# First-pass values of a graph-attention kernel: DVE and ACT in turn on two tiles, POOL left out

## The chip, the cores and the metric

The kernel runs on one core of a Trainium2 chip. The metric is the device time of one execution in microseconds (us). The kernel before takes 3360.18 us, the median of three executions between 3354.19 and 3361.27 us.

The core's engines are TensorE (PE, with its weight loads shown as PEld), VectorE (DVE), ScalarE (ACT), GpSimd (POOL) and SyncE (SP, which only issues DMAs here). They run their own instruction streams and meet at semaphores.

## The reference

Four graph layers over 4096 nodes with 256 features. Layers 0 and 1 are graph attention with four heads of 64 columns; layer 2 is a wide attention with gates; layer 3 is attention with one score per node. Each layer's output is added to `x` and normalised.

```python
h = jnp.einsum('nf,hfd->hnd', x, W)
s_src = jnp.einsum('hnd,hd->hn', h, a1)
s_dst = jnp.einsum('hnd,hd->hn', h, a2)
e = jax.nn.leaky_relu(s_src[:, :, None] + s_dst[:, None, :], 0.01)
e = jnp.where(adj[None, :, :] == 0, -jnp.inf, e)
alpha = jax.nn.softmax(e, axis=-1)
out = jnp.einsum('hij,hjd->hid', alpha, h)
```

A leaky relu of a sum has two exponentials, one for each sign. So the kernel computes the softmax numerator as two masked sums over `j`, one with `exp(s_dst)` where the sum of scores is above zero, one with `exp(slope * s_dst)` where it is not. What is multiplied by the masks, `h` times one of the two exponentials, is called "values" in the kernel. Layer 3 has a single exponential and so one kind of values.

## The kernel before

Nodes are laid out as 128 partitions by T = 32 tiles. Layers 0, 1 and 3 run attention in four passes of 64 columns (`p`), each over eight groups of 512 target nodes (`g`), each in eight units (`k`). Layer 2 (`dense2`) has its own code, which the change does not touch.

**The values.** PE multiplies fp8 masks of zeros and ones by bf16 values. To keep fp32 accuracy each value is split into three bf16 parts. `value_parts` (line 462) makes them for `n` tiles of one kind: copy the exponential beside the products (line 467), multiply `h` by it into `big` (468), cast `big` to the first part (472), subtract it from `big` into `rest` (475), cast `rest` to the second part (478), subtract that into the third part (481). Each step waits for the one before. A chunk is CHUNK = 8 tiles; a kind has FIRST_CHUNKS = 4 chunks. A chunk is 128 x 520 elements.

**Who makes them.** The values of pass 0 cannot be made before the scores and exponentials of the layer exist, so they stand between the dense product and the attention. In layers 0 and 1, DVE makes all four chunks of kind 1 (line 1438) and the last chunk of kind 0 (`rest_of_first_values`, line 1318), with the temporary `vtmp_dve`; POOL makes the other three chunks of kind 0 (`first_values`, line 535, in `vtmp_pool`). In layer 3 DVE makes three chunks and POOL one. `POOL_CHUNKS` holds the split. The values of passes 1 to 3 are made by POOL in the slack of the pass before (line 595, half-size pieces, 128 x 260).

**What starts the attention.** PE waits for DVE's chunks (`s_vfirst`, line 992) and POOL's (`s_vals`, lines 981 and 999), and then for the masks of unit 0 (`s_sides`, line 958). The masks: ACT makes `above` for a unit with four relus (line 760), two units ahead, after copying the pass's scores into `kpass` (line 745); DVE takes the unit's adjacency bits (`edge`, line 1503), ANDs them with `above` (`pos`, 1509) and XORs (`neg`, 1512). In layer 3 there is no `above`; line 1500 makes the whole mask. DVE evacuates the banks of the group before at line 1454; in layer 0's first pass PE waits for that at the first group too, because a single half of the banks is used there and the packing of the adjacency matrix shares the pass. That packing takes six groups: SP loads 1 MB halves of a row block (line 350), DVE converts them (1212), PE packs (945), DVE stores (1218). SP's next load waits for the conversion of the half in the same buffer.

POOL also turns sums into quotients (lines 553 and 568 to 576), after it has made the group's values for the next pass. DVE's evacuation waits for the quotient of a group earlier (line 1451). Before each attention POOL runs one `PARTITION_ALL_REDUCE` (line 533).

The order on every engine is that of the program; there is no planner.

Of the kernel before, what the change touches and what calls it, by code (L numbers as in the profile page):

```python
# [6 lines left out]
ALU = mybir.AluOpType  # L7
# [10 lines left out]
P = 128  # L18
# [5 lines left out]
H = 4  # L24
D = F // H
# [15 lines left out]
POOL_CHUNKS = {0: 3, 1: 3, 3: 1}  # L41
# [17 lines left out]
def values_before(l):  # L59

    return sum(POOL_CHUNKS[m] + (H - 1) * NG for m in TURN if m < l)


def first_values_until(l):

    return sum(FIRST_CHUNKS - POOL_CHUNKS[m] for m in TURN if m <= l)

# [54 lines left out]
def gnn_kernel(nc, A, out, last_layer=3):  # L122

    with ExitStack() as ctx:
# [155 lines left out]
        s_vfirst = sem("dve_values_made")  # L280
        s_vals = sem("values_made")
# [202 lines left out]


        @block.gpsimd
        def _(pool):
# [47 lines left out]
            def first_values(l):  # L535
                if l < 3:
                    pool.wait_ge(s_exps, l + 1)
                else:
                    pool.wait_ge(s_emul, 1)
                with pool.Fori(0, POOL_CHUNKS[l]) as c:  # L540
                    chain.enter(c, VALUE_LINKS)
                    value_parts(pool, chain, vtmp_pool, 0, c * CHUNK, CHUNK, 0, 0).then_inc(s_vals, 1)
                chain.leave(POOL_CHUNKS[l])

# [35 lines left out]
            def attention(l):  # L580
                kinds = 2 if l < 3 else 1
                per_group = VALUE_LINKS * kinds + (3 if l < 3 else 2)
                for p in range(H if l < 3 else H - 1):

                    links = per_group - (0 if p < H - 1 else VALUE_LINKS * kinds)
                    if p < H - 1:

                        pool.wait_ge(s_unit, p * UNITS + (CREDIT + TURN[l] * H * UNITS))
                    with pool.Fori(0, NG // 2) as gg:
                        for par in range(2):  # L590
                            g = gg * 2 + par
                            chain.enter(g, links)
                            if p < H - 1:
                                for kind in range(kinds):
                                    made = value_parts(pool, chain, vtmp_pool, kind, g * GT, GT, p + 1, 1 - p % 2)
                                made.then_inc(s_vals, 1)
                            quotient(l, p, g, par)
                    chain.leave(NG)
# [77 lines left out]
            for l in range(last_layer + 1):  # L676
# [7 lines left out]
                if l != 2:  # L684
                    first_values(l)
                    attention(l)
# [7 lines left out]
        def _(act):  # L694
# [29 lines left out]
            def stats(l):  # L724
# [12 lines left out]
                else:  # L737
                    act.activation(emul[:, 0, 0, :], emul[:, 0, 0, :], ACT.Exp).then_inc(s_exps, 1)

# [147 lines left out]
            for l in range(last_layer + 1):  # L887
# [17 lines left out]
                stats(l)  # L905
                if l < 2:
                    attention(l)
# [8 lines left out]
        def _(pe):  # L916
# [62 lines left out]
            def one_pass(l, slot, p):  # L979

                pe.wait_ge(s_vals, p * NG + (values_before(l) + POOL_CHUNKS[l]))
# [8 lines left out]
            def attention(l):  # L990
# [8 lines left out]
                pe.wait_ge(s_vals, POOL_CHUNKS[0])  # L999
# [181 lines left out]
        def _(dve):  # L1181
# [136 lines left out]
            def rest_of_first_values(l):  # L1318

                with dve.Fori(POOL_CHUNKS[l], FIRST_CHUNKS) as c:  # L1320
                    chain.enter(c - POOL_CHUNKS[l], VALUE_LINKS)
                    value_parts(dve, chain, vtmp_dve, 0, c * CHUNK, CHUNK, 0, 0).then_inc(s_vfirst, 1)
                chain.leave(FIRST_CHUNKS - POOL_CHUNKS[l])
# [75 lines left out]
            def stats(l):  # L1399
# [9 lines left out]
                if l == 3:  # L1409
# [12 lines left out]
                    rest_of_first_values(l)  # L1422
# [15 lines left out]
                with dve.Fori(0, FIRST_CHUNKS) as c:  # L1438
                    chain.enter(c, VALUE_LINKS + 1)
                    value_parts(dve, chain, vtmp_dve, 1, c * CHUNK, CHUNK, 0, 0).then_inc(s_dve, 1)  # L1440
                    dve.wait_ge(s_dve, chain.next())
                chain.leave(FIRST_CHUNKS)
                rest_of_first_values(l)
# [308 lines left out]
```

## Time and profile before

| | us |
|---|---|
| median of three executions | 3360.18 |
| lowest, highest | 3354.19, 3361.27 |
| the profiled execution | 3357.18 |
| its span in the trace | 3355.4 |
| its mean granted TensorE clock | 0.961 |

| engine | busy us | share of the span | instructions |
|---|---|---|---|
| PE | 3011.8 | 90% | 26664 |
| PEld | 2751.1 | 82% | 26664 |
| DVE | 2278.4 | 68% | 4091 |
| ACT | 1914.1 | 57% | 3380 |
| POOL | 1226.3 | 37% | 1640 |

Of the chain of work that ended last, PE has 73% of the span, DVE 15%, issue 5%, DMA 3% and POOL 2%.

In the rows below, "busy" is the time in which an engine worked on an instruction, and the number in brackets is the idle time of the engine just before the instruction, with what ended it. "issue" is idle time in which the engine waited for nothing that the profile shows. Names left and right of "<-" are the tiles written and read; `rings` holds DVE's temporary and the masks, `values` holds the bf16 parts. [...] Times are microseconds from the span's start. The stretches of rows 1 are the first values of layers 0, 1 and 3, from DVE's first copy to its first mask.

### The profile page before, as it was taken

Reading aid. Unit: us, or ns where it says so; the run is one execution under the profiler, and the core shown is the slowest. Engines: PE = TensorE matmul, PEld = TensorE weight load, DVE = VectorE, ACT = ScalarE, POOL = GpSimd, SP = SyncE. Lnnn points to the kernel's source line nnn. Section 1 sums busy time; section 2 is a strip of 40 time slices with the busy share of each in tenths; the row PEclk is TensorE's granted clock in tenths of the full one; section 3 lists DMA queues with packets and bytes.
Section 4 is the critical chain, followed back from the end, with each engine's and each line's share of the span. In section 5 each row is a group of like instructions: output and inputs, shape, how many; then the busy total and the mean of one; then the engine's idle time right before and its main releaser. Section 6 shows DMA issues by size and latency. Waiting matters only on the chain.

```text
span 3355.4 us, 74122 instructions
## 1 busy us (share of the span) xinstructions
PE 3011.8 (90%) x26664; PEld 2751.1 (82%) x26664; DVE 2278.4 (68%) x4091; ACT 1914.1 (57%) x3380; POOL 1226.3 (37%) x1640
## 2 busy tenths in 40 slices
PE   6588899999955999999997999999999998569997
PEld 5587899999945999999995787887887886359997
DVE  4888788887777888888776555655655554454447
ACT  4455798889845898898884454444454443320000
POOL 2433456551214555545212013223223232324443
PEclk9799999999987999999998999999999998789999
DMA  7465000000100000000010000000000000000001
GB/s 258 177 243 205 10 13 11 12 13 13 61 0 11 13 13 11 12 13 10 12 40 7 9 2 4 4 1 4 4 1 4 1 1 2 0 1 0 0 0 50
DMA packets 42286, 104.58 MB, mean 31 GB/s; under 512 B 9904, under 2 KB 23472, under 8 KB 33968
## 3 DMA queue, kind: packets, MB, share of 16 engines
q1 hardware_dynamic: 42160, 102.92, 9.1%
q8 instruction: 77, 1.26, 0.2%
q14 instruction: 49, 0.40, 0.0%
HBM read 98.51 MB, written 4.39 MB: 31 GB/s over the span
## 4 chain that ended last, share of the span: by engine, by line
PE 73%; DVE 15%; issue 5%; DMA 3%; POOL 2%; ACT 1%; DVEq 1%; SPq 0%; POOLq 0%; ACTq 0%
PE bank L970 16%; PE bank L967 16%; PE bank L1014 14%; PE bank L1052 11%; PE bank L973 10%; DVE sums L1454 4%; DVE rings L1509 3%; PE bank L931 2%; DMA arena<-in_adj_dram 2%; DVE rings L1512 2%; PE bank L1041 2%; PE bank L1028 1%; PE bank L945 1%; DVE rings L1503 1%; DVE arena L1212 1%
## 5 line engine op out<-in xcount | busy, mean ns | idle before, releaser
L967 PE MATMUL bank<-values,rings 128*128 128x195 bf16 x8192 | 1418.4, 247 | 138.0 <-DVE rings L1512 79.0
L760 ACT ACTIVATE above<-srow,kpass 128x512 fp8e4<-128x512 f32 x2048 | 1292.9, 709 | 294.3 <-DVE rings L1512 278.6
L970 PE MATMUL bank<-values,rings 128*128 128x195 bf16 x8192 | 1418.6, 249 | 0.0
L967 PEld LDWEIGHTS bank<-values,rings 128*128 128x128 fp8e4 x8192 | 809.2, 99 | 157.2 <-issue 155.8
L970 PEld LDWEIGHTS bank<-values,rings 128*128 128x128 fp8e4 x8192 | 787.1, 96 | 1.1
L1509 DVE TENSOR_TENSOR rings<-rings,above 128x512 uint32<-128x512 uint32 x512 | 385.1, 752 | 237.2 <-PE bank L970 190.5
L778 ACT ACTIVATE values<-srow,cmul 128x512 f32<-128x512 f32 x256 | 205.9, 814 | 433.3 <-PE bank L1052 432.3
L1052 PE MATMUL bank<-hv,values 128*128 128x257 f32 x1792 | 423.8, 382 | 9.5 <-DVE values L1388 9.5
L1512 DVE TENSOR_TENSOR rings<-rings 128x512 uint32<-128x512 uint32 x512 | 408.6, 798 | 17.5
L1052 PEld LDWEIGHTS bank<-hv,values 128*128 128x128 f32 x1792 | 336.9, 191 | 80.5 <-issue 25.5
L973 PE MATMUL bank<-values,rings 128*128 128x195 bf16 x4096 | 349.3, 248 | 23.0 <-DVE rings L1500 23.0
L973 PEld LDWEIGHTS bank<-values,rings 128*128 128x128 fp8e4 x4096 | 348.6, 98 | 23.9 <-issue 23.4
L553 POOL TENSOR_TENSOR quot<-sums,cmul 128x260 f32<-128x260 f32 x64 | 43.8, 684 | 762.0 <-DVE sums L1454 762.0
L1503 DVE TENSOR_SCALAR rings<-packed 128x512 uint32 (+1 forms) x512 | 309.9, 605 | 0.7 <-DVE values L481 0.6
L1500 DVE TENSOR_SCALAR rings<-packed 128x512 uint32 (+1 forms) x256 | 113.3, 443 | 179.7 <-PE bank L973 177.8
L1388 DVE SCALAR_TENSOR_TENSOR values<-values,cmul,rings 128x512 f32<-128x512 f32 x256 | 193.1, 761 | 47.4 <-ACT values L778 46.4
L619 POOL TENSOR_SCALAR zrow<-zrow 128x1 f32<-128x1 f32 x96 | 39.1, 407 | 465.4 <-DVE zrow L1575 465.4
L1454 DVE TENSOR_REDUCE sums<-bank 128x130 f32<-128x390 f32 (+1 forms) x396 | 168.0, 486 | 15.8 <-PE bank L970 14.0
L1014 PE MATMUL bank<-arena,above 128*128 128x256 f32 (+1 forms) x512 | 176.0, 492 | 2.3 <-ACT above L842 2.3
L931 PE MATMUL bank<-weights,values 128*128 128x264 f32 (+1 forms) x512 | 141.8, 437 | 26.3 <-ACT values L699 25.9
L931 PEld LDWEIGHTS bank<-weights,values 128*128 128x128 f32 x512 | 108.8, 218 | 53.7 <-ACT values L699 33.7
L1014 PEld LDWEIGHTS bank<-arena,above 128*128 128x128 f32 x512 | 98.0, 192 | 60.0 <-issue 49.2
(177 smaller groups left out, 3505.4 us busy)
## 6 DMA issues: line engine op xcount, KB each, us to landing
arena<-in_adj_dram SPq DMA_DIRECT2D x64, 1024.0 KB, 5.7
srow<-src_dram SPq DMA_DIRECT2D x72, 256.0 KB, 3.2
x<-in_x_dram SPq DMA_DIRECT2D x1, 4096.0 KB, 14.3
out_dram<-x SPq DMA_DIRECT2D x8, 512.0 KB, 2.9
arena<-in_L_gnn_fe_w_dram SPq DMA_DIRECT2D x2, 512.0 KB, 10.0
arena<-in_L_gnn_W_hz_dram SPq DMA_DIRECT2D x1, 1024.0 KB, 10.4
arena<-in_L_gnn_g_w_dram SPq DMA_DIRECT2D x1, 1024.0 KB, 11.6
weights<-in_L_gnn_W_dram SPq DMA_DIRECT2D x3, 256.0 KB, 3.3
```

The lines of the kernel that those rows point to most:

```text
L760: last = act.activation(above[:, k % 2, q, :], srow[:, par, :], ACT.Relu, scale=BIG, bias=kpass[:, slot, q * BITS + k:q * BITS + k + 1], s ...
L778: act.activation(w2[:, m % DEPTH, :], srow[:, g % 2, :], ACT.Relu, scale=b_col[:, jt:jt + 1], bias=c_neg[:, jt:jt + 1]).then_inc(E.relu, 1)
L931: last = pe.matmul(bank[2 + i][:, 0:width], xT[:, i, k, :], weights[:, k, 0:width], start=(k == 0), stop=(k == 1))
L967: pe.matmul(acc[:, 0:KW], pos[:, k % 2, q, :].bitcast(FP8)[:, rows], v[:, 0:KW], start=first, stop=final, skip_group_check=True)
L970: last = pe.matmul(acc[:, KW:2 * KW], neg[:, k % 2, q, :].bitcast(FP8)[:, rows], v[:, KW:2 * KW], start=False, stop=final, skip_group_chec ...
L973: last = pe.matmul(acc[:, 0:KW], edge[:, k % 2, q, :].bitcast(FP8)[:, rows], v[:, 0:KW], start=first, stop=final)
L1014: last = pe.matmul(dst, lhsT[k], rhs[k], start=(k == 0), stop=(k == len(lhsT) - 1))
L1052: last = pe.matmul(bank[it][:, 0:VW], w2[:, m % DEPTH, it * P:(it + 1) * P], hv[:, q * BITS + k, :], start=(k == 0 and q == 0), stop=False)
L1454: last = dve.tensor_reduce(sums[:, slot, it, 0:kinds, :], parts, AX.X, ALU.add)
L1503: dve.tensor_scalar(edge[:, r], words, shift[0], ONE, shift[1], ALU.bitwise_and)\
L1509: dve.tensor_tensor(pos[:, r], edge[:, r], above[:, r].bitcast(U32), ALU.bitwise_and)\
L1512: dve.tensor_tensor(neg[:, r], edge[:, r], pos[:, r], ALU.bitwise_xor).then_inc(s_sides, 1)
```

## The change

The first pass's values are made without POOL. `first_values` on DVE goes through the chunks in pairs, the even one in `vtmp_dve` and the odd one in `vtmp_pool`, eight chunks (both kinds) in layers 0 and 1 and four in layer 3. DVE copies the exponential, multiplies, and later makes the two subtractions. ACT makes the two casts of each chunk in `first_casts`, between `stats` and `attention` in its program. Three new semaphores carry the turn: `s_vbig` (multiplied), `s_vcast` (cast), `s_vrest` (rest made). The loops over the chunks are written out in Python, so their instructions stand in line instead of in a hardware loop. POOL waits in `attention` for `s_vfirst`, since DVE now uses its temporary. PE waits for `s_vfirst` alone.

```diff
--- before.py
+++ after.py
@@ -38,7 +38,6 @@
 EPS = 1e-5
 CHUNK = 8
 FIRST_CHUNKS = T // CHUNK
-POOL_CHUNKS = {0: 3, 1: 3, 3: 1}
 UNITS = NG * BITS
 PACKED_FIRST = QUADS
 PACKING = (T - PACKED_FIRST) // GT
@@ -58,12 +57,17 @@
 
 def values_before(l):
 
-    return sum(POOL_CHUNKS[m] + (H - 1) * NG for m in TURN if m < l)
+    return sum((H - 1) * NG for m in TURN if m < l)
+
+
+def first_chunks(l):
+
+    return FIRST_CHUNKS * (2 if l < 3 else 1)
 
 
 def first_values_until(l):
 
-    return sum(FIRST_CHUNKS - POOL_CHUNKS[m] for m in TURN if m <= l)
+    return sum(first_chunks(m) for m in TURN if m <= l)
 
 
 
@@ -278,6 +282,7 @@
         s_exps = sem("exps_made")
         s_emul = sem("layer3_weights_made")
         s_vfirst = sem("dve_values_made")
+        s_vbig, s_vcast, s_vrest = sem("values_multiplied"), sem("values_cast"), sem("values_rest")
         s_vals = sem("values_made")
         s_srow = [sem("srow_loaded0"), sem("srow_loaded1")]
         s_above = sem("above_made")
@@ -482,6 +487,14 @@
 
         VALUE_LINKS = 4
 
+        def chunk_of(c):
+
+            return (vtmp_dve, vtmp_pool)[c % 2], c // FIRST_CHUNKS, c % FIRST_CHUNKS * CHUNK
+
+        def first_part(kind, j0, i):
+
+            return values[:, 0, j0:j0 + CHUNK, kind * KW + i * C:kind * KW + (i + 1) * C]
+
 
         @block.gpsimd
         def _(pool):
@@ -531,16 +544,6 @@
                 n = H if l < 2 else 1
                 pool.wait_ge(s_pmax, l + 1)
                 pool.partition_all_reduce(smax[:, 1, 0:n], smax[:, 0, 0:n], P, RMAX).then_inc(s_max, 1)
-
-            def first_values(l):
-                if l < 3:
-                    pool.wait_ge(s_exps, l + 1)
-                else:
-                    pool.wait_ge(s_emul, 1)
-                with pool.Fori(0, POOL_CHUNKS[l]) as c:
-                    chain.enter(c, VALUE_LINKS)
-                    value_parts(pool, chain, vtmp_pool, 0, c * CHUNK, CHUNK, 0, 0).then_inc(s_vals, 1)
-                chain.leave(POOL_CHUNKS[l])
 
             def quotient(l, p, g, par):
 
@@ -580,6 +583,7 @@
             def attention(l):
                 kinds = 2 if l < 3 else 1
                 per_group = VALUE_LINKS * kinds + (3 if l < 3 else 2)
+                pool.wait_ge(s_vfirst, first_values_until(l))
                 for p in range(H if l < 3 else H - 1):
 
                     links = per_group - (0 if p < H - 1 else VALUE_LINKS * kinds)
@@ -682,7 +686,6 @@
                     stage_x()
                 global_max(l)
                 if l != 2:
-                    first_values(l)
                     attention(l)
             if last_layer == 2:
                 dense2()
@@ -736,6 +739,19 @@
                     act.activation(c, c, ACT.Exp).then_inc(s_exps, 1)
                 else:
                     act.activation(emul[:, 0, 0, :], emul[:, 0, 0, :], ACT.Exp).then_inc(s_exps, 1)
+
+            def first_casts(l):
+
+                before = first_values_until(l) - first_chunks(l)
+                for pair in range(0, first_chunks(l), 2):
+                    for c in (pair, pair + 1):
+                        vtmp, kind, j0 = chunk_of(c)
+                        act.wait_ge(s_vbig, before + c + 1)
+                        act.activation(first_part(kind, j0, 0), vtmp[:, 0], ACT.Copy).then_inc(s_vcast, 1)
+                    for c in (pair, pair + 1):
+                        vtmp, kind, j0 = chunk_of(c)
+                        act.wait_ge(s_vrest, before + c + 1)
+                        act.activation(first_part(kind, j0, 1), vtmp[:, 1], ACT.Copy).then_inc(s_vcast, 1)
 
             def attention(l):
 
@@ -903,6 +919,8 @@
                     with act.Fori(0, QUADS) as q:
                         dense(l, q)
                 stats(l)
+                if l != 2:
+                    first_casts(l)
                 if l < 2:
                     attention(l)
             if last_layer == 2:
@@ -978,7 +996,7 @@
 
             def one_pass(l, slot, p):
 
-                pe.wait_ge(s_vals, p * NG + (values_before(l) + POOL_CHUNKS[l]))
+                pe.wait_ge(s_vals, p * NG + values_before(l))
                 pe.nop(nofuse=True)
                 with pe.Fori(0, NG // 2) as gg:
                     for par in range(2):
@@ -996,7 +1014,6 @@
                             one_pass(l, slot, pp * 2 + slot)
                     return
 
-                pe.wait_ge(s_vals, POOL_CHUNKS[0])
                 for begin, end in ((0, PACKING), (PACKING, NG)):
                     with pe.Fori(begin, end) as g:
 
@@ -1315,12 +1332,28 @@
                 dve.tensor_reduce(scores[:, H, ds(q * QT, QT)], low, AX.X, ALU.add).then_inc(s_dve, 1)
                 dve.wait_ge(s_dve, chain.next())
 
-            def rest_of_first_values(l):
-
-                with dve.Fori(POOL_CHUNKS[l], FIRST_CHUNKS) as c:
-                    chain.enter(c - POOL_CHUNKS[l], VALUE_LINKS)
-                    value_parts(dve, chain, vtmp_dve, 0, c * CHUNK, CHUNK, 0, 0).then_inc(s_vfirst, 1)
-                chain.leave(FIRST_CHUNKS - POOL_CHUNKS[l])
+            def first_values(l):
+
+                before = first_values_until(l) - first_chunks(l)
+                for pair in range(0, first_chunks(l), 2):
+                    both = (pair, pair + 1)
+                    for c in both:
+                        vtmp, kind, j0 = chunk_of(c)
+                        big = vtmp[:, 0]
+                        e = emul[:, kind, 0:1, j0:j0 + CHUNK].rearrange("p a n -> p n a")
+                        dve.tensor_copy(big[:, :, D:C], e)
+                        dve.tensor_tensor(big[:, :, 0:D], h[:, j0:j0 + CHUNK, 0:D], e.to_broadcast([P, CHUNK, D]),
+                                          ALU.mult).then_inc(s_vbig, 1)
+                    for c in both:
+                        vtmp, kind, j0 = chunk_of(c)
+                        dve.wait_ge(s_vcast, 2 * (before + c - c % 2) + c % 2 + 1)
+                        dve.tensor_tensor(vtmp[:, 1], vtmp[:, 0], first_part(kind, j0, 0), ALU.subtract)\
+                            .then_inc(s_vrest, 1)
+                    for c in both:
+                        vtmp, kind, j0 = chunk_of(c)
+                        dve.wait_ge(s_vcast, 2 * (before + c - c % 2) + c % 2 + 3)
+                        dve.tensor_tensor(first_part(kind, j0, 2), vtmp[:, 1], first_part(kind, j0, 1), ALU.subtract)\
+                            .then_inc(s_vfirst, 1)
 
                 dve.wait_ge(s_vfirst, first_values_until(l))
 
@@ -1419,7 +1452,7 @@
                     dve.tensor_copy(emul[:, 0, 0, :], emul[:, 0, 1, :]).then_inc(s_emul, 1)
                     chain.settle()
                     dve.wait_ge(s_emul, 1)
-                    rest_of_first_values(l)
+                    first_values(l)
                     return
 
                 z, az, m = (zrow[:, i] for i in range(3))
@@ -1435,12 +1468,7 @@
                 chain.settle()
 
                 dve.wait_ge(s_exps, l + 1)
-                with dve.Fori(0, FIRST_CHUNKS) as c:
-                    chain.enter(c, VALUE_LINKS + 1)
-                    value_parts(dve, chain, vtmp_dve, 1, c * CHUNK, CHUNK, 0, 0).then_inc(s_dve, 1)
-                    dve.wait_ge(s_dve, chain.next())
-                chain.leave(FIRST_CHUNKS)
-                rest_of_first_values(l)
+                first_values(l)
 
             def evacuate(l, half, slot, count):
```

## Rows read from the trace of the kernel before

**Rows 1.** By stretch: length, busy PE, PEld, DVE, ACT, POOL; clock, DMA share, GB/s.
```profile
84.35:110.55 26.20, 0.00 (x0) 0.00 (x0) 20.69 (x30) 5.01 (x8) 13.44 (x15) 0.50 0.24 92
1022.23:1048.64 26.41, 0.00 (x0) 0.00 (x0) 21.19 (x30) 5.01 (x8) 15.78 (x17) 0.50 0.07 20
2974.46:2988.65 14.19, 0.00 (x0) 0.00 (x0) 11.52 (x19) 0.00 (x0) 6.60 (x8) 0.50 0.00 0
```

**Rows 2.** Timeline (start, duration, engine, line, operation), layer 0, DVE's first chunk.
```profile
84.35 0.17 DVE L467 COPY rings<-emul 128x8 f32 x1 [1.09 <-ACT cmul L736]
...
84.50 0.69 DVE L468 TENSOR_TENSOR rings<-hv,emul 128x512 f32 x1
85.41 0.43 DVE L472 CAST values<-rings 128x520 f32 x1 [0.22 <-DVE rings L468]
...
85.95 0.70 DVE L475 TENSOR_TENSOR rings<-rings,values 128x520 f32<-128x520 f32 x1
```

**Rows 3.** Timeline, layer 1, DVE and POOL both making values.
```profile
1040.16 1.14 POOL L475 TENSOR_TENSOR vtmp_pool<-vtmp_pool,values 128x520 f32<-128x520 f32 x1
1040.50 1.36 DVE L481 TENSOR_TENSOR values<-rings,values 128x520 f32 x1 [0.20 <-DVE values L478]
```

**Rows 4.** Instructions of ACT by line and shape (busy us, mean ns): nearest to a cast.
```profile
L760 ACT ACTIVATE above<-srow,kpass 128x512 fp8e4<-128x512 f32 x2048 | 1292.9, 709 | 294.3 <-DVE rings L1512 278.6 <-DMA srow<-src_dram 4.3 <-ACT kpass L745 3.4
...
L868 ACT ACTIVATE values<-values 128x512 f32<-128x512 f32 x16 | 9.9, 618 | 15.4 <-DVE values L1688 15.4
...
L704 ACT ACTIVATE x<-values 128x1024 f32<-128x1024 f32 x2 | 2.1, 1048 | 0.0
```

**Rows 5.** Timeline, layer 3: DVE to ACT and back.
```profile
2973.06 0.19 DVE L1408 TENSOR_TENSOR emul<-scores,smax 128x32 f32<-128x32 f32 x1 [0.55 <-POOL smax L533]
...
2973.29 0.23 ACT L738 ACTIVATE emul<-emul 128x32 f32<-128x32 f32 x1 [3.51 <-DVE emul L1408]
2973.62 0.40 DVE L1416 TENSOR_TENSOR emul<-emul,zrow 128x32 f32<-128x32 f32 x3 [0.28 <-ACT emul L738]
```

**Rows 6.** Waits of ACT (total us, times, longest), relus after the kpass copy.
```profile
ACT above L760 <- ACT kpass L745: 3.4, 6, 0.6
```

**Rows 7.** Timeline of ACT, layer 0: four relus of one unit.
```profile
113.75 2.56 ACT L760 ACTIVATE above<-srow,kpass 128x512 fp8e4<-128x512 f32 x4 [22.89 <-DVE rings L1512]
```

**Rows 8.** Timeline, layer 0, from the values to PE.
```profile
111.28 1.35 DVE L1509 TENSOR_TENSOR rings<-rings,above 128x512 uint32<-128x512 uint32 x1 [0.21 <-DVE rings L1503]
...
113.58 1.96 DVE L1454 TENSOR_REDUCE sums<-bank 128x130 f32<-128x390 f32 x4
...
115.89 0.32 PE L967 MATMUL bank<-values,rings 128*128 128x195 bf16 x1 [35.56 <-DVE sums L1454]
```

**Rows 9.** Timeline, layer 1, from the values to PE.
```profile
1049.28 1.45 DVE L1509 TENSOR_TENSOR rings<-rings,above 128x512 uint32<-128x512 uint32 x1 [0.21 <-DVE rings L1503]
...
1052.04 0.32 PE L967 MATMUL bank<-values,rings 128*128 128x195 bf16 x1 [33.13 <-DVE rings L1512]
```

**Rows 10.** Timeline of DVE, layer 1, masks with POOL nearly quiet.
```profile
1057.00 0.69 DVE L1509 TENSOR_TENSOR rings<-rings,above 128x512 uint32<-128x512 uint32 x1 [0.45 <-ACT above L760]
1057.72 0.77 DVE L1512 TENSOR_TENSOR rings<-rings 128x512 uint32<-128x512 uint32 x1
```

**Rows 11.** Timeline, layer 3, from the values to PE.
```profile
2988.65 0.97 DVE L1500 TENSOR_SCALAR rings<-packed 128x512 uint32 x2 [0.60 <-DVE values L481]
...
2989.22 5.95 PE L973 MATMUL bank<-values,rings 128*128 128x195 bf16 x36 [23.03 <-DVE rings L1500]
```

**Rows 12.** Timeline of SP, layer 0, first loads after the values.
```profile
116.85 20.34 SPq L350 DMA_DIRECT2D arena<-in_adj_dram  x6
```

**Rows 13.** Waits of POOL (total us, times, longest).
```profile
POOL quot L568 <- DVE sums L1454: 165.3, 32, 12.7
...
POOL vtmp_pool L468 <- issue: 25.9, 5, 10.6
```

**Rows 14.** Waits of DVE on nothing that the profile shows.
```profile
DVE lnst L1250 <- issue: 3.8, 1, 3.8
```

## Prediction, made before the changed kernel was run

> **What bounds the kernel now.** I read the chain of work that ended last first: PE has 73% of the span and DVE only 15%, so making DVE cheaper is worth nothing inside a pass. Then the busy time by stretch. In three stretches PE has no matmul at all: 26.20 us in layer 0, 26.41 us in layer 1 and 14.19 us in layer 3 [rows 1]. These are the first pass's values, and nothing else is ready for PE. DVE is busy for 20.69, 21.19 and 11.52 us of them, so what ends them is DVE's own series of steps. Whatever is cut from DVE's series, up to PE's first matmul, is cut from the time, and the stretches occur once each. Last, the timeline shows what stands between DVE's last value and PE: PE begins at 115.89, 1052.04 and 2989.22 [rows 8, 9, 11], which is 31.54, 29.81 and 14.76 us after DVE's first copy (84.35, 1022.23 and 2974.46, the starts of the stretches in [rows 1]).
>
> **Prices of the steps.** On DVE a copy starts at 84.35 and its multiply at 84.50, ends at 85.19; a subtraction is 0.70 and a cast 0.43 [rows 2]. That is DVE without POOL. With POOL at work a subtraction took 1.36 beside POOL's 1.14 [rows 3]; this extra goes, since POOL makes nothing in the stretch. Instructions that don't depend on each other overlap a little: ACT's four relus of 0.709 need 2.56 instead of 2.84 [rows 4, 7], 0.09 less at each seam. I take 0.08 on DVE too and, at the far end, zero. ACT's cast isn't in the trace. 128 x 512 without a per-partition bias is 0.618 and 128 x 1024 is 1.048 [rows 4]; 520 elements come to 0.62 us. The bounds are 0.43 (DVE's own cast) and 0.71 (a relu with its bias [rows 4]). A hand-over: DVE ends at 2973.25, ACT starts at 2973.29; ACT ends at 2973.52, DVE starts at 2973.62 [rows 5]. So 0.04 and 0.10, and 0.57 (3.4 / 6 [rows 6]) as the far end. I take 0.04 to 0.06, as loops and their register work fall away.
>
> **A pair of chunks, step by step.** From its first copy at 0: multiplies end at 0.84 and 1.59. ACT casts 0.88 to 1.50 and 1.63 to 2.25. DVE subtracts 1.56 to 2.26 and 2.31 to 3.01. ACT casts the rests 2.30 to 2.92 and 3.05 to 3.67. DVE subtracts the third parts 2.98 to 3.68 and 3.73 to 4.43. The next pair starts at 4.35; I take 4.4 a pair. DVE has 3.9 us of work in it, so little is left to win; ACT has 2.5. Layers 0 and 1 have four pairs: DVE ends at 3 x 4.4 + 4.43 = 17.6, ACT's last cast at 3 x 4.4 + 3.67 = 16.9. Layer 3 has two: DVE ends at 8.8.
>
> **The wait that the change adds.** ACT's casts stand ahead of its relus. Before, ACT made eight relus for units 0 and 1 (5.01 us [rows 1]) while DVE made values; they cost nothing. Behind the last cast now stand the kpass copy and the relus of unit 0, and DVE's `pos` waits for them. 16.87, 0.2 for the copy, 0.57 to the first relu [rows 6], 2.56 for four [rows 7]: `pos` starts at 20.2 instead of 17.6 + 1.0. This costs 1.6 us in each of layers 0 and 1. The relus of unit 1 end at 22.8; `pos` of unit 1 wants them only after unit 0's matmuls are under way, so they stay hidden. Before, `pos` started at 111.28 - 84.35 = 26.93 and 1049.28 - 1022.23 = 27.05.
>
> **From the masks to PE.** `pos` and `neg` take 0.69 and 0.77 with POOL quiet, 1.49 from start to end [rows 10]; before, `pos` alone was 1.35 and 1.45 beside POOL [rows 8, 9]. Layer 1: 20.2 + 1.49 = 21.7 instead of 29.81, 8.1 us won. Layer 0: DVE also evacuates first; from that instruction's start (113.58) to PE is 2.31, so 21.6 + 2.3 = 23.9 instead of 31.54, 7.6 us won. Layer 3: no relus; 8.83 + 0.60 + 0.57 [rows 11] = 10.0 instead of 14.76, 4.8 us won.
>
> **Whether it is carried to the end.** After the values of layer 0 the adjacency loads set the pace, but SP's next load was issued at 116.85, after DVE's first conversion [rows 12], so the stream of loads starts earlier with DVE. After that every stage waits for the one before. I find no absolute time in the program.
>
> **What moves on POOL.** POOL now waits for `s_vfirst`, and behind that stand the values of pass 1 and the quotients. Its first multiply after the all-reduce waits for nothing visible, 10.6 us at the longest, 25.9 in all [rows 13]. Before, this ran beside DVE's values; now it starts after them. In layers 0 and 1 POOL is then at its pass-1 values at 17.6 + 10.6 = 28.2 or earlier, about when it got there before, when it had three chunks to make first. In layer 3 it is about 16, 6 us after PE's start. There POOL idles 165.3 / 32 = 5.2 us in each group before a quotient [rows 13], and that quotient is wanted a group later. So I cost it at nothing; if the cover were gone, it would be up to 3 us in layer 3. [...]
>
> **The sum.** 7.6 + 8.1 + 4.8 = 20.5 us. The profiled execution took 3357.18 (span 3355.4 and 1.8 around it), 3.0 under the median of the three. From the profiled execution it is 3336.7, from the median 3339.7. I say 3338.5, 0.65% less.
>
> **Own range of the forecast.** A pair could be 4.2 (casts at 0.43 leave DVE's own work and the hand-overs) or 5.2 (casts at 0.71 and 0.15 more in each of four hand-overs). Three pairs and a tail in two layers, two in the third: some ten pairs' worth, less for the smaller steps. That is 2 us more or 8 us less won: 3334.7 to 3344.7 from the profiled execution, up to 3347.7 from the median.
>
> **Rivals.** *Hand-overs as dear as the dearest.* Four hand-overs of 0.57 in a pair [rows 6] make it 6.4 us. Three pairs and three hand-overs more cost 7.5 us in each of layers 0 and 1, and 4 us in layer 3: 19 of the 20.5 are gone, 3355.7 to 3358. For it: it is a real row. Against it: that row has a loop's register work in it, and [rows 5] cross between the same two engines at 0.04 and 0.10. Chance 0.07.
> *Layer 0's share isn't carried.* If the load stream, not DVE, sets the end of the first pass, 7.6 us are lost: 3344 to 3347. For it: the loads set the pace there. Against it: their start follows DVE. Chance 0.10.
> *No overlap.* If the two chunks of a pair really run in series, a chunk is 0.84 + 2 x 0.62 + 2 x 0.70 + 4 x 0.05 = 3.7 us; eight are 29.6, and with the relus behind them PE starts 5.4 - 1.0 us later in two layers and 1.1 in layer 3: 10 us slower, 3367 to 3370. This is also where the change wouldn't do what it says. Against it: the program's order interleaves them. Chance 0.02.
> [...] Chance 0.05. [...]
>
> **How the numbers follow.** The forecast has 0.76, the rivals 0.07, 0.10, 0.02 and 0.05. A measurement of this kernel tells some 0.2% (6.7 us) from no change. Faster: 0.76 + 0.10 = 0.86. Same: 0.07. Slower: 0.07. The range is 3331 to 3349: the forecast's own range from both bases, 3 us wider below, and it holds the second rival.
>
> **What would show it.** In the timeline of the changed kernel: pairs of 4.4 us; ACT casts of 0.62; DVE subtractions of 0.70 all through; `pos` of unit 0 ending a wait for ACT's relu in layers 0 and 1; PE's first matmul 23.9, 21.7 and 10.0 us after DVE's first copy; POOL's stall of 7 to 11 us after that, without anybody behind it. The forecast is wrong if casts are over 0.8 us, if DVE stands between the steps for more than 0.3, or if PE waits for sums that wait for POOL.

## The result, and the profile after

The changed kernel takes 3335.36 us (median of four, 3329.51 to 3337.34) where the kernel before took 3358.14 us in the same session. The ratio is 0.993 with a 95% interval of 0.9912 to 0.9948: 22.8 us less. Run once more in another session it took 3334.19 against 3356.62, ratio 0.9938 (0.9924 to 0.9951). All times here and below are medians of the executions, without a single one of 5385.11 us of the run "POOL kept busy", in which the granted clock was 0.556.

The page's engines and its chain of work that ended last. POOL made 42 instructions fewer, ACT 40 more; DVE's count is the same but for two.

```profile
PE 3012.7 (90%) x26664; PEld 2751.2 (82%) x26664; DVE 2266.7 (68%) x4093; ACT 1939.8 (58%) x3420; POOL 1188.9 (36%) x1598
...
PE 73%; DVE 14%; issue 6%; DMA 3%; ACT 2%; POOL 2%; DVEq 1%; SPq 0%; POOLq 0%; ACTq 0%
```

The shares say little: they are those of before within a point or two. The change is in three short stretches, which answer to [rows 1] (columns as there).

```profile
84.87:101.88 17.01, 0.00 (x0) 0.00 (x0) 16.48 (x32) 10.67 (x18) 0.00 (x0) 0.50 0.40 145
1015.65:1032.81 17.16, 0.00 (x0) 0.00 (x0) 16.49 (x32) 10.83 (x18) 0.12 (x1) 0.50 0.11 31
2959.92:2968.97 9.05, 0.00 (x0) 0.00 (x0) 8.29 (x17) 5.15 (x8) 0.19 (x1) 0.50 0.00 0
```

They are 9.2, 9.2 and 5.1 us shorter, and DVE is busy for 16.48 of 17.01 us, where it was busy for 20.69 of 26.20. POOL has left them. One pair of chunks in the timeline of layer 1:

```profile
1015.65 0.18 DVE L1344 COPY rings<-emul 128x8 f32<-128x8 f32 x1 [0.88 <-ACT cmul L739]
1015.73 0.69 DVE L1345 TENSOR_TENSOR rings<-hv,emul 128x512 f32<-128x512 f32 x1
1016.33 0.17 DVE L1344 COPY vtmp_pool<-emul 128x8 f32<-128x8 f32 x1
1016.40 0.68 DVE L1345 TENSOR_TENSOR vtmp_pool<-hv,emul 128x512 f32<-128x512 f32 x1
1016.45 0.65 ACT L750 ACTIVATE values<-rings 128x520 bf16<-128x520 f32 x1 [0.83 <-DVE rings L1345]
1017.12 0.65 ACT L750 ACTIVATE values<-vtmp_pool 128x520 bf16<-128x520 f32 x1
1017.13 0.70 DVE L1350 TENSOR_TENSOR rings<-rings,values 128x520 f32<-128x520 f32 x1
1017.80 0.70 DVE L1350 TENSOR_TENSOR vtmp_pool<-vtmp_pool,values 128x520 f32<-128x520 f32 x1
1017.87 0.64 ACT L754 ACTIVATE values<-rings 128x520 bf16<-128x520 f32 x1
1018.54 0.64 ACT L754 ACTIVATE values<-vtmp_pool 128x520 bf16<-128x520 f32 x1
1018.54 0.70 DVE L1355 TENSOR_TENSOR values<-rings,values 128x520 bf16<-128x520 f32 x1
1019.21 0.70 DVE L1355 TENSOR_TENSOR values<-vtmp_pool,values 128x520 bf16<-128x520 f32 x1
1019.83 0.17 DVE L1344 COPY rings<-emul 128x8 f32<-128x8 f32 x1
```

DVE has next to no idle time between these rows, and the next pair starts after 4.18 us. ACT has a part in the pace: its casts of a pair start 0.67 us apart, and each of DVE's subtractions starts 0.03 us after the end of the cast that it needs (1017.10 and 1017.13, 1017.77 and 1017.80). So the two engines go in step, each with 0.64 to 0.70 us per instruction. The end of the same stretch, with the wait that the change adds:

```profile
1031.59 0.21 ACT L761 ACTIVATE kpass<-kscores 128x32 f32 x1
...
1032.38 9.91 ACT L776 ACTIVATE above<-srow,kpass 128x512 fp8e4<-128x512 f32 x16 [0.58 <-ACT kpass L761]
...
1032.81 0.43 DVE L1531 TENSOR_SCALAR rings<-packed 128x512 uint32 x1 [0.39 <-DVE values L1355]
1034.97 0.69 DVE L1537 TENSOR_TENSOR rings<-rings,above 128x512 uint32<-128x512 uint32 x1 [1.73 <-ACT above L776]
```

DVE has its bits at 1033.24 and waits 1.73 us for ACT's relus; before, the same instruction had its usual 0.21 [rows 9]. PE's first matmuls of layers 0, 1 and 3, each from the timeline of PE:

```profile
107.85 0.32 PE L985 MATMUL bank<-values,rings 128*128 128x195 bf16 x1 [26.79 <-DVE sums L1482]
```
```profile
1036.53 0.32 PE L985 MATMUL bank<-values,rings 128*128 128x195 bf16 x1 [24.01 <-DVE rings L1540]
```
```profile
2969.54 2.77 PE L991 MATMUL bank<-values,rings 128*128 128x195 bf16 x16 [17.69 <-DVE rings L1528]
```

From DVE's first copy that is 22.98, 20.88 and 9.62 us, where it was 31.54, 29.81 and 14.76 [rows 8, 9, 11]. This number, "PE's start", is what I compare from here on.

### The profile page after: what moved, and what is told of

The parts are those of the page before. It is cut to its first block, busy times and chain, and to the rows that moved or that the text cites. A ratio compares the mean times of both kernels' runs of the same rounds, so it can differ in the third digit from the quotient of the medians.

```text
span 3335.5 us, 73845 instructions
## 1 busy us (share of the span) xinstructions
PE 3012.7 (90%) x26664; PEld 2751.2 (82%) x26664; DVE 2266.7 (68%) x4093; ACT 1939.8 (58%) x3420; POOL 1188.9 (36%) x1598
## 4 chain that ended last, share of the span: by engine, by line
PE 73%; DVE 14%; issue 6%; DMA 3%; ACT 2%; POOL 2%; DVEq 1%; SPq 0%; POOLq 0%; ACTq 0%
PE bank L988 16%; PE bank L985 16%; PE bank L1031 14%; PE bank L1069 11%; PE bank L991 10%; DVE sums L1482 4%; DVE rings L1537 3%; DMA arena<-in_adj_dram 2%; DVE rings L1540 2%; PE bank L1058 2%; PE bank L949 1%; PE bank L1045 1%; DVE rings L1531 1%; DVE arena L1229 1%; PE bank L963 1%
```

## The experiments

The table has PE's start in microseconds in each kernel's trace, the sum over the three layers against before (76.1), and the time against the kernel before on the same chip.

| kernel | layer 0 | layer 1 | layer 3 | sum | sum against before | time against before |
|---|---|---|---|---|---|---|
| before, first and second trace | 31.54, 31.54 | 29.81, 29.79 | 14.76, 14.75 | 76.1 | | |
| changed, first and second trace | 22.98, 22.97 | 20.88, 20.87 | 9.62, 9.62 | 53.5 | -22.6 | -22.8, -22.4 |
| all on DVE, pairs | 25.21 | 23.28 | 11.93 | 60.4 | -15.7 | -16.7 |
| all on DVE, old loops | 36.51 | 34.78 | 15.84 | 87.1 | +11.0 | +10.6 |
| POOL keeps its chunks | 31.34 | 28.66 | 13.74 | 73.7 | -2.4 | -2.6 |
| one chunk at a time | 34.25 | 32.15 | 15.25 | 81.7 | +5.5 | +4.7 |
| POOL kept busy | 28.76 | 26.71 | 10.98 | 66.5 | -9.7 | -13.2 |
| POOL warmed up | 23.10 | 21.01 | 9.89 | 54.0 | -22.1 | -22.2 |
| relus in ACT's gaps | 21.30 | 19.36 | 9.62 | 50.3 | -25.8 | -26.5 |

**Casts on DVE too.** ACT's `first_casts` goes; DVE makes the casts in the same pairs.

```diff
+for c in both:
+    dve.wait_ge(s_vbig, before + c + 1)
+    dve.tensor_copy(first_part(kind, j0, 0), vtmp[:, 0]).then_inc(s_vcast, 1)
...
-    first_casts(l)
```

> POOL makes no first values, as in the changed kernel, but DVE makes the casts too and ACT none. Theory (the change is two gains that add: POOL out of the way, casts off DVE): a pair of chunks is 4.17 + 4 x 0.35 = 5.6 us; ACT's relus are hidden again. PE starts 24.9 us after DVE's first copy in layer 1, 27.0 in layer 0, 12.4 in layer 3, which is 10.8 us in all more than in the changed kernel and 11.8 less than in the kernel before. Rival 1 (the casts on ACT are the whole gain): the time of the kernel before, 22 us over the changed one. Rival 2 (POOL's quiet is the whole gain): within 3 us of the changed kernel.

Measured: 3339.74 against 3356.46, ratio 0.9947 (0.9931 to 0.9964). Both rivals fall, and the theory's split is wrong in size: 4 to 6 us over the changed kernel by the times and 6.9 by PE's starts, not 10.8. In its timeline (layer 0) DVE shows no idle time and casts follow each other after 0.34 us:

```profile
86.06 0.42 DVE L1348 CAST values<-rings 128x520 bf16<-128x520 f32 x1
86.40 0.42 DVE L1348 CAST values<-vtmp_pool 128x520 bf16<-128x520 f32 x1
...
86.74 0.69 DVE L1352 TENSOR_TENSOR rings<-rings,values 128x520 f32<-128x520 f32 x1
87.35 0.69 DVE L1352 TENSOR_TENSOR vtmp_pool<-vtmp_pool,values 128x520 f32<-128x520 f32 x1
```

Its subtractions start 0.61 apart, where in the changed kernel they follow ACT's casts and start 0.67 apart, so a pair takes 5.16 and not 5.6. The casts on ACT shorten the stretch by 4 us in each of layers 0 and 1, of which the relus behind them take back 1.7 and 1.5.

**The old loops on DVE, POOL out.** The kernel before, with `POOL_CHUNKS` at zero and POOL waiting for `s_vfirst`. DVE has the same work as in the run above, in hardware loops, one step behind the other.

```diff
-POOL_CHUNKS = {0: 3, 1: 3, 3: 1}
+POOL_CHUNKS = {0: 0, 1: 0, 3: 0}
...
+pool.wait_ge(s_vfirst, first_values_until(l))
```

> The kernel before with one edit: DVE makes all chunks (eight, four in layer 3) in its old hardware loops, one step waiting for the other, and POOL makes none and waits for the values, as in the changed kernel. With the run in which DVE did everything in pairs written out, this parts POOL's quiet from the order of the steps. In the trace of before, chunks of kind 1 without POOL took 4.5, 4.3, 4.25 and 4.2 us in the loop, those of layer 3 3.65. Theory A (the order of the steps and the missing loop are the larger part): the values take about 32 us in layers 0 and 1 and 14.6 in layer 3; PE starts about 36.8, 33.7 and 15.8 us after DVE's first copy, 10 us in all later than in the kernel before and 26 later than with the pairs written out on DVE alone. Rival B (POOL's quiet is what the gain came from): at least as fast as the kernel before, PE's starts within 2 us in all of 60.4, those of the pairs on DVE alone.

Measured: 3366.92 against 3356.37, ratio 1.0028 (1.0014 to 1.0042), and PE's starts within 1.1 us of theory A. Rival B falls. One chunk in layer 0:

```profile
84.60 0.43 DVE L472 CAST values<-rings 128x520 f32 x1 [0.22 <-DVE rings L468]
85.14 0.70 DVE L475 TENSOR_TENSOR rings<-rings,values 128x520 f32<-128x520 f32 x1
86.05 0.43 DVE L478 CAST values<-rings 128x520 f32 x1 [0.21 <-DVE rings L475]
86.74 0.70 DVE L481 TENSOR_TENSOR values<-rings,values 128x520 f32 x1 [0.26 <-DVE values L478]
88.03 0.18 DVE L467 COPY rings<-emul 128x8 f32 x1 [0.59 <-DVE values L481]
```

The durations are those of the pairs; what differs is 0.20 to 0.26 us in front of three of the dependent steps, 0.1 in front of the subtraction behind the first cast, and 0.59 at the turn. Eight chunks take 32.2 us in this form and 20.9 in pairs written out, with the same work and with POOL quiet in both.

The 0.59 isn't a price of the turn as such. The loop of kind 1 waits at its end for its last subtraction (`dve.wait_ge(s_dve, chain.next())` in the kernel before), and its turns show 0.40 to 0.59. The loop of kind 0 doesn't wait there, and its next copy starts before the last subtraction has ended, as it does in all turns of layer 3:

```profile
103.94 0.70 DVE L481 TENSOR_TENSOR values<-rings,values 128x520 f32 x1 [0.20 <-DVE values L478]
104.56 0.17 DVE L467 COPY rings<-emul 128x8 f32 x1
```

A chunk takes 4.2 to 4.3 us on the average in the loop with that wait and 3.65 in the one without (3.84 in layer 1). The 0.2 us in front of dependent steps isn't a price of the dependence alone either. Where DVE waits for its own last result in straight code, it starts 0.03 to 0.04 us after the end, as in the kernel before (layer 0):

```profile
82.04 0.23 DVE L1428 TENSOR_SCALAR zrow<-zrow 128x128 f32<-128x128 f32 x1
82.30 0.29 DVE L1430 TENSOR_TENSOR zrow<-zrow 128x128 f32<-128x128 f32 x1
```

And in layer 3 the first copy of the values waits for the same step in both kernels: 0.23 us in the kernel before, where a loop begins there, and 0.03 in the changed one:

```profile
2959.71 0.18 DVE L1452 COPY emul<-emul 128x32 f32<-128x32 f32 x1
2959.92 0.18 DVE L1344 COPY rings<-emul 128x8 f32<-128x8 f32 x1
```

In the loop each such wait compares with a value from a register and has a `nop` behind it (`value_parts`); whether either of the two costs the time no run shows. No run makes the chunks one after the other in straight code on DVE alone. An estimate from these rows, with 0.03 us at each of its four waits, is 3.07 us a chunk, against 3.65 in the loop and 2.58 in pairs. By it the 26.7 us between this run and the one above would be some 5 for the wait at the turn, 12 for the loop's waits and 10 for the two chunks in turn. The run shows the sum; the split is an estimate.

**POOL keeps its chunks.** DVE and ACT take turns on the other five (three), in two tiles (the second is a piece of `rings`, since POOL has `vtmp_pool`); POOL's loop is as before.

```diff
+POOL_CHUNKS = {0: 3, 1: 3, 3: 1}
-return FIRST_CHUNKS * (2 if l < 3 else 1)
+return FIRST_CHUNKS * (2 if l < 3 else 1) - POOL_CHUNKS[l]
...
+with pool.Fori(0, POOL_CHUNKS[l]) as c:
+    value_parts(pool, chain, vtmp_pool, 0, c * CHUNK, CHUNK, 0, 0).then_inc(s_vals, 1)
```

> POOL keeps its three chunks (one in layer 3) as in the kernel before; ACT casts for DVE's other five (three), in turn on two tiles. Theory (POOL was as late as DVE, in layer 1 it ended its third chunk 27.96 us after DVE's first copy): DVE is done at 12 us, PE waits for POOL and starts 27 to 28 us after the first copy in layer 1, 29.7 in layer 0, 13.2 in layer 3: 5 to 6 us less than the kernel before, some 16 more than the changed one. Rival (DVE's own series sets the end whatever POOL does): 20 us or more less than the kernel before.

Measured: 3353.88 against 3356.46, ratio 0.9996 (0.9978 to 1.0013), not told from no change by the times; the trace shows 2.4 us. DVE is done and PE waits for POOL (layer 1, timelines of the engines and of PE):

```profile
1034.07 0.43 DVE L1546 TENSOR_SCALAR rings<-packed 128x512 uint32 x1 [0.39 <-DVE values L1370]
...
1047.56 1.14 POOL L488 TENSOR_TENSOR values<-vtmp_pool,values 128x520 f32 x1 [0.31 <-POOL values L485]
...
1049.45 0.32 PE L999 MATMUL bank<-values,rings 128*128 128x195 bf16 x1 [31.79 <-POOL values L488]
```

The rival falls. The theory has the right wait but not the size: it said 5 to 6 us, and PE started 31.34, 28.66 and 13.74 us after the first copy where it had 29.7, 27 to 28 and 13.2. DVE's masks of unit 0 were ready some 12 us before PE started in layer 1. So in the kernel before, POOL was nearly as late as DVE, and relieving DVE alone brings 2.4 us, where the whole change brings 22.6.

**One chunk at a time.** The changed kernel with `both = (pair,)` on DVE and on ACT.

```diff
-for pair in range(0, first_chunks(l), 2):
-    both = (pair, pair + 1)
+for pair in range(0, first_chunks(l)):
+    both = (pair,)
```

> One chunk at a time instead of two in turn: multiply, cast, subtract, cast, subtract, then the next chunk. Each engine waits for the other. Theory (the turn on two tiles hides the casts): a chunk is 3.5 us, eight are 27.8 and four 13.9; PE starts 11 us later than in the changed kernel in layers 0 and 1 and 5.5 in layer 3, 27 to 28 us in all, so that it is some 5 us slower than the kernel before. Rival (the gain is from less work on DVE, in whatever order): within 5 us of the changed kernel.

Measured: 3361.19 against 3356.46, ratio 1.0015 (1.0006 to 1.0025). PE's starts are 11.3, 11.3 and 5.6 us later than in the changed kernel, as the theory says. Each engine waits for the other, 0.7 us at a time (layer 0):

```profile
84.28 0.65 ACT L750 ACTIVATE values<-rings 128x520 bf16<-128x520 f32 x1 [0.83 <-DVE rings L1345]
84.96 0.70 DVE L1350 TENSOR_TENSOR rings<-rings,values 128x520 f32<-128x520 f32 x1 [0.72 <-ACT values L750]
85.69 0.64 ACT L754 ACTIVATE values<-rings 128x520 bf16<-128x520 f32 x1 [0.77 <-DVE rings L1350]
```

**POOL kept busy.** Throwaway subtractions on POOL in its own scratch while the values are made.

```diff
+pool.memset(quot[:, 0:2], 1.0).then_inc(s_pool, 1)
+pool.wait_ge(s_pool, chain.next())
+for _ in range(12 if l < 3 else 4):
+    pool.tensor_tensor(quot[:, 2], quot[:, 0], quot[:, 1], ALU.subtract).then_inc(s_pool, 1)
+    pool.wait_ge(s_pool, chain.next())
```

> As the changed kernel, but POOL makes twelve throwaway subtractions of 128 x 260 (four in layer 3) into its own scratch while DVE and ACT make the values. Nothing waits for them. Theory (half of the gain is that POOL is out of DVE's way): DVE's subtractions go from 0.70 to between 1.0 and 1.4 us while POOL works, the stretches grow by 4 to 8 us in layers 0 and 1 and by 1 to 3 in layer 3, in all 9 to 19 us more than the changed kernel. Rival (the two don't disturb each other, the casts were everything): DVE stays at 0.70 and the time within 2 us of the changed kernel.

Measured: 3343.47 against 3356.62, ratio 0.9966 (0.9953 to 0.9979): 9 us over the changed kernel, 13.0 by PE's starts (5.8, 5.8 and 1.4), both within what the theory says. The rival falls. In layer 0:

```profile
89.74 13.89 POOL L551 TENSOR_TENSOR quot<-quot 128x260 f32<-128x260 f32 x12 [8.13 <-issue]
...
93.52 0.70 DVE L1351 COPY rings<-emul 128x8 f32<-128x8 f32 x1
94.12 0.68 DVE L1352 TENSOR_TENSOR rings<-hv,emul 128x512 f32<-128x512 f32 x1
...
95.94 1.23 DVE L1357 TENSOR_TENSOR rings<-rings,values 128x520 f32<-128x520 f32 x1
...
97.09 1.23 DVE L1357 TENSOR_TENSOR vtmp_pool<-vtmp_pool,values 128x520 f32<-128x520 f32 x1
```

Subtractions take 1.23 instead of 0.70 and the small copy 0.70 instead of 0.17; each is longer by 0.53. POOL's twelve took 1.16 us each, where one takes 0.66 in the first row of the next run, so POOL was slowed as well. From one of DVE's subtractions to the next it is 1.15 us, close to POOL's 1.16; why, no row shows. POOL worked without a break here, so this is not what its three chunks cost DVE in the kernel before; no run has that alone.

**POOL warmed up.** One throwaway product on POOL right after the all-reduce.

```diff
+pool.tensor_tensor(credits[:, 14:15], minus_half, minus_half, ALU.mult)
```

> POOL makes one throwaway product of 128 x 1 right after the all-reduce, so that its stall of 7 us runs beside DVE's values and not after them. Theory A (nobody waits for POOL's late start; it even keeps POOL off DVE's first masks): POOL's first values now lie beside pos and neg of unit 0, which take 2.4 us again instead of 1.4; PE starts 1 us later in layers 0 and 1, 0.2 in layer 3: 2 us more than the changed kernel. Rival B (the late start costs what the packed groups lost): the packed groups are 1.6 us shorter, and the time is the same or less.

Measured: 3334.41 against 3356.62, ratio 0.9935 (0.992 to 0.995), the changed kernel's time. Theory A's price was wrong: POOL does start 7 us earlier, beside the first masks, but these took 0.73 and 0.77 us and not 2.4 together, and PE's starts moved by 0.13, 0.13 and 0.27.

```profile
103.39 0.66 POOL L480 TENSOR_TENSOR vtmp_pool<-vtmp_pool,values 128x260 f32<-128x260 f32 x1 [0.16 <-POOL values L477]
103.86 0.73 DVE L1539 TENSOR_TENSOR rings<-rings,above 128x512 uint32<-128x512 uint32 x1 [1.89 <-ACT above L778]
104.26 0.59 POOL L483 CAST values<-vtmp_pool 128x260 f32 x1 [0.22 <-POOL vtmp_pool L480]
104.63 0.77 DVE L1542 TENSOR_TENSOR rings<-rings 128x512 uint32<-128x512 uint32 x1
```

Its packed groups (first to seventh evacuation) took 215.3 us against 217.9 and 216.4 in the two traces of the changed kernel. That speaks for a part of rival B; the next two runs show how far such lengths vary by themselves.

**The two kernels once more**, for what varies by itself.

> The changed kernel once more, for how far the length of a stage varies between two executions of the same program. In its first profile PE's first matmul of the attention came 22.98, 20.88 and 9.62 us after DVE's first copy of the values in layers 0, 1 and 3; these three should repeat within 0.3 us. From PE's first matmul of layer 0 to the evacuation that ends the packed groups it had 1.6 us more than the kernel before, and layer 2 had 1.5 us more. If those are chance (loads and long chains), they come out elsewhere here; if they are a price of the change (POOL starting later), they repeat within 0.5 us.

> The kernel before once more, for its trace alone. PE's starts after DVE's first copy should be 31.5, 29.8 and 14.8 us again within 0.5 (POOL and DVE meet by chance, so they may vary more than in the changed kernel). The packed groups of layer 0 (first evacuation to the seventh) took 216.3 us in its first profile and 215.0 to 217.9 in the runs without POOL's early start; if these differences are chance, it comes out within 2 us of 216 here as well.

Measured: PE's starts repeated within 0.02 us in both kernels. The packed groups took 216.3 and 215.6 in the kernel before, 217.9 and 216.4 in the changed one, and between 214.5 and 216.8 in six of the experiments (in the seventh, where POOL keeps its chunks, the first evacuation lies far ahead of PE's start and isn't comparable). Layer 2, from the last evacuation of layer 1 on the chain to DVE's first copy of layer 3, took 1196.1, 1197.7 and 1195.8 us in before, changed and changed again. So the 1.5 us in layer 2 don't repeat and are chance. Of the 1.6 us in the packed groups 0.1 to 0.7 are left in the second trace. A part may be POOL's: where its stall was over before PE started (before twice, POOL warmed up, POOL kept busy) the packed groups took 214.5 to 216.3 us, and where it came after (changed twice and four experiments) 216.0 to 217.9. The means lie 1.2 us apart and the ranges overlap, so a price of about a microsecond for POOL's late start is likely and not shown.

**Relus in ACT's gaps.** ACT idles 1.44 us after each pair. Two relus go there, and the first pass is written out of ACT's loop with units 0 and 1 of its first group left out.

```diff
+act.activation(kpass[:, 0:1, :], kscores[:, 0:1, :], ACT.Copy).then_inc(s_kpass, 1)
...
+for q in (pair % 4, pair % 4 + 1):
+    last = act.activation(above[:, k, q, :], srow[:, 0, :], ACT.Relu, scale=BIG,
+                          bias=kpass[:, 0, q * BITS + k:q * BITS + k + 1], saturate=False)
```

> ACT idles 1.44 us after each pair of chunks. Here it uses this for the relus of units 0 and 1 of the first group (two after each pair), so that they no longer stand behind the last cast; the first pass is taken out of ACT's loop for it. Theory (the relus are what PE's start waits for): pos of unit 0 begins 0.6 us after edge instead of 2.3 and 2.2, PE starts 1.7 us earlier in layer 0 and 1.5 in layer 1, layer 3 stays: 3.2 us less than the changed kernel. Rival (ACT's idle time is too short, casts are late): pairs grow from 4.17 to 4.5 us or more and the gain is under 1.5 us.

Measured: 3330.14 against 3356.62, ratio 0.9925 (0.9911 to 0.9938), 4.0 us under the changed kernel in the same session; by PE's starts 3.2, as expected. The rival falls: two relus take 1.32 us and the next cast begins 0.22 after them, with pairs of 4.17. In layer 1 (timeline of ACT, then DVE):

```profile
1016.99 1.32 ACT L765 ACTIVATE above<-srow,kpass 128x512 fp8e4<-128x512 f32 x2
1018.53 0.65 ACT L752 ACTIVATE values<-rings 128x520 bf16<-128x520 f32 x1 [0.22 <-DVE rings L1366]
```
```profile
1030.72 0.43 DVE L1552 TENSOR_SCALAR rings<-packed 128x512 uint32 x1 [0.39 <-DVE values L1376]
1031.36 0.69 DVE L1558 TENSOR_TENSOR rings<-rings,above 128x512 uint32<-128x512 uint32 x1 [0.21 <-DVE rings L1552]
```

The wait of 1.73 us has become 0.21. This is the fastest kernel of the study.

## Why the prediction was right, point by point

**What bounds.** Right. The three stretches without PE were the place, and the time fell by what PE's starts fell: 22.6 us by the traces, 22.8 by the times. I had said 20.5. The time itself, 3335.36 where I had 3338.5, is 3.1 us lower: 2.3 from the sum (by the times), the rest from the base, which I took between the profiled execution and a median that came out 2 us lower with more executions.

**Prices.** The cast took 0.64 to 0.65, I had 0.62. Hand-overs were 0.03 in both directions (DVE ends at 1016.42, ACT starts at 1016.45; ACT ends at 1017.10, DVE starts at 1017.13), I had 0.04 to 0.06.

**A pair.** The term that was mis-sized: 4.17 us instead of 4.4. I let the second multiply end at 1.59; it ended at 1.43, since each copy delays its multiply by 0.07 or 0.08 and not 0.15, and everything behind follows; the rest is that I rounded 4.35 up. Four pairs: 17.0 instead of 18.0 to the first mask, two: 9.05 instead of 9.4. This is most of the 2.1 us that the sum lacks.

**The added wait.** Right in place and near in size: I had 1.6 us, it was 1.7 in layer 0 and 1.5 in layer 1 (1.89 and 1.73 less the usual 0.2), and filling ACT's gaps gave it back.

**From the masks to PE.** 0.69 and 0.69 as soon as POOL is away. PE's starts were 22.98, 20.88 and 9.62 where I had 23.9, 21.7 and 10.0; the gains 8.6, 8.9 and 5.1 where I had 7.6, 8.1 and 4.8.

**Carried to the end.** Right within what the stages vary by themselves. The rival that layer 0's share is lost didn't come: by the clock of the trace PE started 8.0 us earlier in the first trace and 8.5 in the second (115.89 against 107.85 and 107.44), and the evacuation of the eighth group lay 6.4 and 8.7 us earlier (357.27 against 350.84 and 348.53).

**POOL.** Costed at nothing, and the times show nothing; the packed groups leave room for about a microsecond. Its stall came where I had put it, at 6.95, 7.18 and 6.81 us, shorter than the 10.6 taken for layer 0, so POOL reached pass 1 at 24.4 and not 28. Warming it up left the time as it was: 22.2 us under the kernel before, where the changed kernel is 22.8 and 22.4 under it.

**The other rivals.** No overlap: the run with one chunk at a time gives its price, PE's starts 5.5 us later than before in all; I had 10; a chunk took 3.5 us and not 3.7, which makes 4 us over the twenty chunks. The dear hand-overs aren't in the trace. The last chance in the list, 0.05, stood for a slower kernel, by a stall of 3.8 us at each turn of a loop. No run shows such turns: in the changed kernel DVE stood idle twice without a visible wait, 3.8 and 0.2 us, as in the kernel before, and the time fell by 22.8 us.

**What I had not seen.** The prediction counts the new form only, and so never asked which edit brings the gain. The runs part it, in this order: taking POOL's chunks away in the old form costs 11.0 us; writing the steps out in pairs on DVE brings 26.7; the casts on ACT bring 6.9 (10.1 with the relus in ACT's gaps). 11.0 - 26.7 - 6.9 = -22.6. In another order the parts would differ: ACT's casts and the pairs brought only 2.4 us as long as POOL kept its chunks. I had written that POOL's extra "goes", which is true (1.36 to 0.70 on a subtraction), but POOL also carried three of eight chunks, and its absence is a cost until the idle gaps between DVE's steps are closed.

## What to carry to other kernels

In a short serial stretch before the matmuls, count the gaps between dependent steps, and look for a wait at the turn of the loop, before moving work to another engine: two independent pieces in turn, written out and without that wait, brought 26.7 us where the casts on ACT brought 6.9. An engine that helps must be looked at for when it ends, not for how much it does: freeing DVE alone brought 2.4 us, because POOL ended as late. Work put in front of an engine's next duty shows up as a wait there; look for idle slots inside the stretch and put that duty into them.

## What the runs showed of the hardware

POOL and DVE slow each other: with POOL subtracting without a break, DVE's two-operand 128 x 520 subtraction took 1.23 us instead of 0.70, a 128 x 8 copy 0.70 instead of 0.17, the multiply right behind the copy nothing more, and POOL's 128 x 260 subtraction 1.16 from one to the next instead of 0.66 for one. A uint32 AND beside POOL's subtraction and cast took 0.73 instead of 0.69.

POOL's first two-operand instruction after the all-reduce came 6.75 to 10.6 us after the end of the copy, memset or all-reduce in front of it, with no wait that the profile shows, in each of three layers and wherever the code put it. The product that warmed it up took this stall upon itself, 7.19, 7.29 and 6.99 us, and POOL's first multiply of the values behind it had none. What POOL does in it no run here shows.

In the hardware loops that make the values DVE stood idle for 0.19 to 0.29 us (once 0.56) before most steps that waited for the one before and for 0.1 before the others, and in straight code for 0.03 to 0.04. The turn of a loop showed 0.40 to 0.59 us where the code waits for the last step there, and nothing where it doesn't. Independent subtractions on DVE started 0.61 us apart at 0.69 us each.
